# Overlapping the edges of two transformer layers: the hand-overs between tile loop, chunk loop, next layer and output

## What is computed

```
h = layernorm(x) * (1 + cb) + sb                  # x: 4 x 1024 x 256
for l in range(2):
    t = shift_token(h)                            # half of the columns come from the row before
    q, k, v = split(t @ wqkv[l])                  # 8 heads of 64, l2-normalised, scaled, rotated
    h = h + local_attention(q, k, v) @ wo[l]      # window 128: own tile of 128 rows and the one before
    t = layernorm(shift_token(h)) * lg + lb
    a, g = split(t @ w1[l] + b1[l])
    h = h + (a * gelu(g)) @ w2[l] + b2[l]
out = x + gb * h
```

## Time and profile before

| | us |
|---|---|
| median of 3 runs (2423.75 to 2428.22) | 2425.5 |
| the profiled execution: its time | 2426.99 |
| the profiled execution: its span | 2425.2 |
| TensorE busy | 2288.2 |
| VectorE busy | 1957.4 |
| ScalarE busy | 1551.4 |
| GpSimd busy | 604.0 |

### The profile page before, as it was taken

One profiled execution on the slowest core, in us unless ns is written; L12 is line 12 of the kernel. 1 busy time (PEld: TensorE's weight loads), 2 busy tenths in 40 slices (PEclk: granted clock), 3 DMA queues, 4 the chain that ended last, 5 costly groups with the idle time before them and its releaser, 6 DMA issues. The chain is left out here.

```text
span 2425.2 us, 63570 instructions
## 1 busy us (share of the span) xinstructions
PE 2288.2 (94%) x21268; PEld 1753.3 (72%) x21268; DVE 1957.4 (81%) x4606; ACT 1551.4 (64%) x3018; POOL 604.0 (25%) x692
## 2 busy tenths in 40 slices
PE   6999999999999999699999997999899999998994
PEld 4767776676777776577777776888677777776884
DVE  6999799979998998688888886666788888885666
ACT  5777577757776775377777674443677777773442
POOL 1000000000000000255555552222545454551110
PEclk9999999999999999899999998999999999998997
DMA  4000100010011001200000000001000000000004
GB/s 130 29 19 13 59 14 19 13 59 21 13 48 49 14 13 45 94 1 2 7 5 4 7 1 28 27 0 40 8 0 9 0 9 0 9 0 10 0 0 139
DMA packets 66986, 58.06 MB, mean 24 GB/s; under 512 B 3812, under 2 KB 64348, under 8 KB 66656
## 3 DMA queue, kind: packets, MB, share of 16 engines
q1 hardware_dynamic: 66912, 57.07, 7.5%
HBM read 44.47 MB, written 8.40 MB: 22 GB/s over the span
## 5 line engine op out<-in xcount | busy, mean ns | idle before, releaser
L599 ACT ACTIVATE at_p<-at_ps_s,at_shift 128x1024 f32<-128x1024 f32 (+3 forms) x384 | 335.7, 899 | 91.2 <-PE at_ps_s L800 49.9
L340 DVE TENSOR_TENSOR at_p_lo<-at_p,at_p_hi 128x1024 f16<-128x1024 f32 (+3 forms) x384 | 357.2, 951 | 5.5
L1355 ACT ACTIVATE ly_probs<-ly_masked,ly_small,ly_rq 128x256 f32<-128x256 f32 x512 | 301.4, 594 | 2.6 <-DVE ly_small L1549 1.4
L828 PE MATMUL at_ps_o<-at_v,at_p_hi 128*128 128x65 f16 x2304 | 238.1, 193 | 3.4 <-DVE at_p_lo L340 2.5
L1249 POOL TENSOR_TENSOR ly_rope_a<-ly_rope_a,ly_rope_t 128x512 f32<-128x512 f32 x132 | 168.8, 1278 | 285.5 <-DVE ly_rope_t L1517 285.5
L828 PEld LDWEIGHTS at_ps_o<-at_v,at_p_hi 128*128 128x128 f16 x2304 | 210.6, 96 | 39.7 <-issue 27.2
L829 PE MATMUL at_ps_o<-at_v,at_p_hi 128*128 128x64 f16 x2304 | 237.2, 194 | 0.0
L830 PE MATMUL at_ps_o<-at_v,at_p_lo 128*128 128x65 f16 x2304 | 236.1, 192 | 0.0
L335 DVE CAST at_p_hi<-at_p 128x1024 f16<-128x1024 f32 (+3 forms) x384 | 206.5, 556 | 25.8 <-ACT at_p L599 14.3
L1363 ACT ACTIVATE ly_operands_plain<-ly_ps 128x512 f32<-128x512 f32 x256 | 152.5, 596 | 102.5 <-PE ly_ps L1773 99.2
L830 PEld LDWEIGHTS at_ps_o<-at_v,at_p_lo 128*128 128x128 f16 x2304 | 212.4, 99 | 0.0
(11 more groups left out here) (238 smaller groups left out, 6242.2 us busy)
## 6 DMA issues: line engine op xcount, KB each, us to landing
at_w_raw<-in_Wv SPq DMA_DIRECT2D x32, 128.0 KB, 2.1
at_w_raw<-in_Wq SPq DMA_DIRECT2D x32, 128.0 KB, 2.3
at_w_raw<-in_Wk SPq DMA_DIRECT2D x32, 128.0 KB, 2.3
at_xio<-in_states SPq DMA_DIRECT2D x4, 1024.0 KB, 6.4
out_x<-x SPq DMA_DIRECT2D x4, 1024.0 KB, 9.5
out<-stream SPq DMA_DIRECT2D x4, 1024.0 KB, 7.9
ly_shifted<-stream SPq DMA_DIRECT2D x8, 508.0 KB
x<-at_xio SPq DMA_DIRECT2D x3, 1024.0 KB, 4.4
```

The lines of the kernel that those rows point to most:

```text
L340: dve.tensor_tensor(p_lo[u % P_RING][:, :, off:], probs[u % P_RING][:, :, off:], p_hi[u % P_RING][:, :, off:], ALU.subtract).then_inc(p_lo ...
L599: act.activation(probs[u % P_RING][:, :, off:], ps_s[u % 2][:, :, off:], ACT.Exp, bias=shift[:], scale=SCORE_SCALE).then_inc(exp_done, 1)
L828: pe.matmul(out, ph, ones_hi, start=(kt == 0 and t == 0), stop=False, skip_group_check=True)
L1355: step = act.activation(pr[:, j % 2, h, :], sm[:, j % 2, h, :], ACT.Exp, bias=small[:, j % 2, 1, h:h + 1], scale=rq[:, par, 2 * j + h:2 * ...
```

## The change

- The wrapped look-ahead goes: tiles 28 to 31 are written out after the loop without the work for tiles past 31 (`left` counts the tiles that follow), tiles 0 and 1 (TensorE: 0 to 3) ahead of it, the first without an output projection.
- Statistics, normalisation, transposes and the first up product of chunk 0 are put inside tiles 29 to 31; the last output projection stands inside chunk 0, between its second and third up product.
- The next layer's first transposes and projections are put inside the last chunk. Chunks 0 and 7 are written out.
- In the tile, the output projection stands ahead of the first transposes of probabilities, values 0 and 1 stand side by side, values 2 and 3 around the next tile's scores; on VectorE the reciprocals stand ahead of the keys' copy.
- A dummy exp follows the last gelu of a layer, a dummy gelu the last exp. At the start, TensorE, VectorE and ScalarE no longer wait for GpSimd's zeroing.
- `phase_output` goes. In layer 1 GpSimd gates the stream and adds the saved x per chunk, VectorE gates the down product from PSUM and adds it, and each half chunk (256 KB) is stored at once. Loads of the saved x go through a ring of three chunks. Layer 1's chunks are written out on VectorE and GpSimd.
- w1 is loaded when the last up product of the layer before is done, wo and w2 when its last down product is. Layer 1's attention weights are split in 6 pieces instead of 8.

The core of the diff (the removed `phase_output`, the indices without look-ahead, and the buffers' places are left out):

```diff
@@ TensorE, tile
-                            project(l, t + 2, par, 2)
-                            scores(l, t, 2, par)
-                            scores(l, t, 3, par)
-                            probs_T(g, 0)
-                            project_out(l, t - 1)
-                            probs_T(g, 1)
-                            project(l, t + 2, par, 1)
-                            values(g, 0, v_slots)
-                            qk_T(l, t + 1, 0)
-                            project(l, t + 2, par, 0)
-                            probs_T(g, 2)
-                            qk_T(l, t + 1, 1)
-                            stream_T(l, t + 3, 1 - par)
-                            values(g, 1, v_slots)
-                            probs_T(g, 3)
-                            scores(l, t + 1, 0, 1 - par)
-                            scores(l, t + 1, 1, 1 - par)
-                            values(g, 2, v_slots)
-                            values(g, 3, v_slots)
-                            reciprocals_T(g)
+                    if left >= 2:
+                        project(l, t + 2, par, 2)
+                    scores(l, t, 2, par)
+                    scores(l, t, 3, par)
+                    if not first:
+                        project_out(l, t - 1)
+                    probs_T(g, 0)
+                    if left >= 2:
+                        project(l, t + 2, par, 1)
+                    probs_T(g, 1)
+                    if left >= 1:
+                        after(pe, "xa_done", g)
+                        qk_T(l, t + 1, 0)
+                    if left >= 2:
+                        project(l, t + 2, par, 0)
+                    probs_T(g, 2)
+                    if left == 0:
+                        after(pe, "f_lo", nth_norm(l, 0) + 1)
+                        hidden(nth_norm(l, 0) * HT, 0, 0)
+                    values(g, 0, v_slots)
+                    values(g, 1, v_slots)
+                    if left >= 1:
+                        qk_T(l, t + 1, 1)
+                    if left >= 3:
+                        stream_T(l, t + 3, 1 - par)
+                    if left == 1:
+                        chunk_T(l, 0, bank[0:2])
+                    probs_T(g, 3)
+                    values(g, 2, v_slots)
+                    if left >= 1:
+                        after(pe, "kT_done", nth(l, t + 1) + 1)
+                        scores(l, t + 1, 0, 1 - par)
+                        scores(l, t + 1, 1, 1 - par)
+                    values(g, 3, v_slots)
+                    reciprocals_T(g)
@@ TensorE, first and last chunk
+                def first_chunk(l):
+                    n = nth_norm(l, 0) * HT
+                    hidden(n, 1, 0)
+                    project_out(l, NT - 1)
+                    hidden(n, 2, 0)
+                    after(pe, "xa_done", NT * (l + 1))
+                    hidden_out(n, 0)
+                    hidden(n, 3, 0)
+                    hidden(n, 4, 0)
+                    chunk_T(l, 1, bank[4:6])
+                    hidden_rest(n, 0)
+                    for i in range(1, HT):
+                        hidden_out(n, i)
+                def last_chunk(l):                          # ... of layer 0
+                    hidden(n, 3, par)
+                    stream_T(l + 1, 0, 0, bank[4])
+                    stream_T(l + 1, 1, 1, bank[5])
+                    hidden(n, 4, par)
+                    hidden_rest(n, par)
+                    hidden_out(n, 1)
+                    after(pe, "gl_done", n + HT - 1)
+                    project(l + 1, 0, 0, 2)
+                    hidden_out(n, 2)
+                    after(pe, "uf_done", n + HT)
+                    project(l + 1, 0, 0, 1)
+                    hidden_out(n, 3)
+                    project(l + 1, 0, 0, 0)
+                    hidden_out(n, 4)
+                    project(l + 1, 1, 1, 2)
+                    hidden_out(n, 5)
+                    after(pe, "ya_done", NCH * (l + 1))
+                    qk_T(l + 1, 0, 0)
...
@@ VectorE
+                def tile(l, t, par, w, pair, left=NT, first=False):
+                    if left >= 1:
+                        rotate_q(l, t + 1, w)
+                        normalise_keys(l, t + 1)
+                    maxima(l, t, 2, par)
+                    if not first:
+                        add_attended(l, t - 1)
+                    if left >= 1:
+                        rotate_k(l, t + 1, w)
+                    maxima(l, t, 3, par)
...
+                    if left == 0:
+                        chunk_lo(l, 0, 0)
+                    reciprocal_sums(nth(l, t), par)
+                    if left >= 1:
+                        copy_keys(l, t + 1, 1 - par)
...
+                    if left == 2:
+                        chunk_statistics(l, 0)
+                        chunk_variance(l, 0)
+                    if left == 1:
+                        chunk_shift(l, 0)
+                        chunk_normalise(l, 0)
+                    if left >= 1:
+                        maxima(l, t + 1, 0, 1 - par)
+                        maxima(l, t + 1, 1, 1 - par)
+                    normalise_out(l, t)
+                def add_hidden(l, c):                       # ... in layer 1
+                    dve.tensor_tensor(g[0], halves[0][1], gate, ALU.mult).then_inc(s["yg_done"], 1)
+                    dve.tensor_tensor(g[1], halves[1][1], gate, ALU.mult).then_inc(s["ya_done"], 1)
+                    dve.wait_ge(s["z_done"], c + 1)
+                    dve.tensor_tensor(halves[0][0], halves[0][0], g[0], ALU.add).then_inc(s["out_done"], 1)
+                    dve.tensor_tensor(halves[1][0], halves[1][0], g[1], ALU.add).then_inc(s["out_done"], 1)
@@ ScalarE, tile
+                    if left == 0:
+                        chunk_hi(l, 0, 0, bank[0:2])        # behind exps(0)
...
+                    if left == 0:                           # behind exps(3)
+                        act.activation(warm[:], expo[:, 0:1], ACT.Gelu).then_inc(s["warmed"], 1)
...
+                    if left == 1:                           # at the tile's end
+                        chunk_full(l, 0, bank[0:2])
@@ ScalarE, last chunk of layer 0, behind the last gelu
+                    act.activation(warm[:], expo[:, 0:1], ACT.Exp).then_inc(s["warmed"], 1)
@@ GpSimd, chunk, layer 1
+                    pool.tensor_tensor(rest, rest, gate, ALU.mult).then_inc(s["z_gated"], 1)
+                    pool.tensor_tensor(rest, rest, x1[:, c % X1_RING], ALU.add).then_inc(s["z_done"], 1)
@@ SyncE, behind layer 1
+                    for i in range(2):
+                        sp.wait_ge(s["out_done"], 2 * c + i + 1)
+                        sp.dma_start(rows_out(c)[:, part, :], x[:, c * CT + 2 * i:c * CT + 2 * i + 2, :]).then_inc(s["stored"], 16)
```

More of the change, by code:

```diff
@@ L1318, in _ @@
[L1318 to L1320 removed]
+                        carry_out(l, 1, 1, 1)
+                        hold(pool, s["tick"], (s["xT_mm"], at(2)))
+                        stage_tile(1, 3)
+                        add_rotated(l, 0, 1)
+                        inverse_key_norms(l, 1)
@@ new lines, in last_chunk @@
+                def last_chunk(l):
+                    n = (l * NCH + NCH - 1) * HT
+                    more = l + 1 < L
+                    for i in range(3):
+                        hidden_full(n, i)
+                        hidden_lo(n, i)
+                    hidden_full(n, 3)
+                    if more:
+                        stream_lo(l + 1, 0, 0, bank[4])
+                    hidden_lo(n, 3)
+                    if more:
+                        stream_lo(l + 1, 1, 1, bank[5])
+                    hidden_full(n, 4)
+                    hidden_full(n, 5)
+                    hidden_lo(n, 4)
+                    hidden_lo(n, 5)
+                    if not more:
+                        add_hidden(l, NCH - 1)
+                        return
+                    l = l + 1
@@ new lines, in last_chunk @@
+                    maxima(l, 0, 0, 0)
+                    maxima(l, 0, 1, 0)
+                for i in range(2):
+                    part = slice(i * A_COLS // 2, (i + 1) * A_COLS // 2)
+                    after(dve, "w_hi_done", i + 1)
+                    dve.tensor_tensor(a_lo[:, part], a_raw[:, part], f32(a_hi[:, part]), ALU.subtract).then_inc(s["w_lo_done"], 1)
+                stream_lo(0, 0, 0)
+                scale_rotations()
+                last_statistics()
+                squared_norms(0, 0, 1)
@@ new lines, in chunk @@
+                def chunk(l, c, par):
+                    ci = nth_norm(l, c)
+                    after(pe, "f_lo", ci + 1)
+                    for i in range(3):
+                        hidden(ci * HT, i, par)
+                    after(pe, "ya_done", ci)
+                    hidden_out(ci * HT, 0)
+                    hidden(ci * HT, 3, par)
+                    hidden(ci * HT, 4, par)
+                    chunk_T(l, c + 1, bank[4:6])
+                    hidden_rest(ci * HT, par)
+                    for i in range(1, HT):
```

(21 more changed lines are left out.)

832 lines of the change are left out of this document (439 added, 393 removed).

## The result

The kernel after takes 2385.4 us (median of 4 runs, 2384.2 to 2386.0), the kernel before 2424.6 in the same session: a ratio of 0.984 (95% interval 0.9825 to 0.9851), 39 us less. I had forecast 2341, with a range of 2318 to 2362. The sign is right; less than half of the gain is there, and the time lies 23 us above the range.

A forecast was written before the change was run, and what follows sets the result against it. TensorE, busy 94% of the span, was taken to bound the kernel, with idle stretches at hand-overs and the end. Terms by stretch summed to -85.2 us from 2427.0, giving 2341.8 (2340 against the median); forecast 2341, range 2318 to 2362.

The forecast's parts named there:

- start, with tile 0: Kernel start: engines no longer wait for GpSimd's zeroing, but most of the gain is lost; 1 us less, bounds 0 and 3.
- order in a tile: 58 whole tiles: eight changes of TensorE array form instead of nine, 0.16 us a tile, 9.3 us less.
- table loads: Layer 1's tile loop: ScalarE's function table load leaves the loop's body, 15 x 1.09 = 16.4 us less.
- tiles to chunks, twice: Tile 29 to chunk 0's end, each layer: 84.9 us falls by 12.5, so 25 less for two.
- layer 0 to layer 1: Start of chunk 7 to end of layer 1's tile 0: 63.9 us becomes 53.4, 10.5 less; bounds 6 and 16.
- layer 1, chunks 1 to 6: VectorE's added additions and GpSimd's passes delay the first down product: 0.35 x 7 = 2.5 us more; bounds 0 and 8.
- last chunk: Layer 1's last chunk: its look-ahead transposes go, 0.8 us less.
- end: Behind the last down product: 31.3 us becomes 6.6, 24.7 less; bounds 21 and 26.
- A: Hand-overs from tiles to chunks hide well: 24 us less a layer instead of 12.5, so 2318 us; chance 0.12.
- B: Hand-overs hide badly, or the tile order gains nothing: +7.5 us a layer and +9.3, so 2365 us; chance 0.14.
- C: The change doesn't do away with layer 1's table loads: 2341 + 16.4 = 2357 us; chance 0.05.
- D: In tiles, the ring of scores, maxima, exps, reciprocals, keys' copy becomes the bound: 15.8 us a tile, 2456 us; chance 0.03.

The follow-up runs named there:

- the loads ahead: Kernel after, with SyncE issuing the next attention weights' loads and x1's loads ahead of the last batch's copy to the shifted stream: 2348.3 us, ratio 0.969.
- the two moves here: On the loads ahead: VectorE's chunk 0 statistics behind tile 30's maxima, 2351.8 us; with GpSimd's passes early too: chunk 0's transposes at tile 30's end, 2338.8 us.

## Why the prediction was wrong

The terms of the sum against what the two traces give, from the same anchors (start of a tile's first projection, start of a chunk):

| term | forecast | measured |
|---|---|---|
| start, with tile 0 | -1.0 | 0.0 |
| order in a tile | -9.3 | -5.8 |
| table loads | -16.4 | -15.5 |
| tiles to chunks, twice | -25.0 | -21.5 |
| layer 0, chunks 1 to 6 | 0 | +15.1 |
| layer 0 to layer 1 | -10.5 | -12.3 |
| layer 1, chunks 1 to 6 | +2.5 | +25.1 |
| last chunk | -0.8 | -1.1 |
| end | -24.7 | -25.9 |
| sum | -85.2 | -41.9 |

**The step that failed** is the one on what is moved to GpSimd and SyncE. I wrote that the gates and additions "go elsewhere", to GpSimd "with 24 us of room", and counted instructions. I never asked when the operand x1 lands, nor that chunk 1 of layer 0 would come 12 us earlier than the loads that GpSimd waits for in it. Both loads stand on SyncE behind the last copy to `shifted`. The windows of the earlier trace rows don't show it, since in the kernel before TensorE did not wait; but GpSimd's timeline did, with 23.6 us of waiting for `in_qk_rows`. In the sum, layer 0's chunks 1 to 6 stand at nothing and layer 1's at +2.5. The step costs 36.2 us (17.0 and 19.2). With the loads ahead the time is 2348.3, inside the range and 7 above the forecast.

**The rest**, term by term.

- Layer 1's chunks: the place was right, and so was the rule of the Trainium skill (page "GPSIMD Engine Reference", section Specifications) that spoke against the change; the size was wrong. I took 0.35 us from one instruction stretched from 0.69 to 1.04; beside two passes back to back the stretch is 1.9 us, and the chunk 1.17 longer than layer 0's, 7 us in all. Moving the passes got it back.
- The chunks' missing 0.31 us (about 5 us) is the operands' offset, which I saw in the diff and priced at nothing.
- Order in a tile: 0.10, not 0.16. I gave every change of form the same 0.15 us. But leaving the scores costs 0.10 us ahead of the output projection (1.83 us for it, and 1.73 behind transposes) and 0.05 ahead of transposes (0.49 for 0.44): putting the projection there gives back most of the missing 0.06.
- Table loads: confirmed alone, at 16.3 us.
- End: four instructions of VectorE, and a span that ends 5.5 us behind the last product, for 6.6; 256 KB land in 2.2 us, for my 2.6.
- Hand-over to the chunks: tile 29 took 13.8 us (13.6 laid out), tile 30 21.6 and 19.8 (18.2), tile 31 17.0 and 16.8 (15.3), chunk 0 22.8 and 24.5 (23.4): the waits are where I put them, and the clock costs more than the 2 us I gave it (in tile 30 of layer 0 eight scores take 2.0 us, and 1.06 elsewhere).
- Hand-over to layer 1: 1.8 us better than laid out, a granted clock of 1.00 throughout.
- Start: TensorE was 1.6 us earlier, and tile 0 took 18.6 instead of 17.0, at a granted clock of 0.82 for 0.90. That VectorE's work for the last batch, which did not move, holds it up is likely and untested.
- The bounds: "the added bounds of the forecast alone are 2322 to 2358" does not come out of the terms. Their own bounds, added one to one, give 2303 to 2396, and the measured time lies inside; the range was narrower than the working behind it.

**Rivals.** A, B and C rested on the hand-overs and the table; none of them describes what happened. B's time is nearer, by accident. D (a ring in the tile) did not occur: the tile has no wait. But the run with the old order on TensorE alone shows how near it was: 0.3 us a tile, most likely from one late copy.

## What to carry to other kernels

When work is pulled forward, look up for each of its operands when it is issued, not only who computes it, and read the whole queue that issues it, also where its waits cost nothing now. A DMA whose issue takes 25 us is a fault even while it is free. A wait that is moved in a chain shared by three engines can come back elsewhere, and with it a lower clock: of the two moves here one cost 3.5 us, the other gained 2.9 in one layer and lost 2.5 in the other. Passes that were moved away from an instruction that TensorE waits for paid in full.

## What the runs showed of the hardware

- A copy of 127 partitions x 8 rows of 512 bytes between two SBUF tensors runs at 20 GB/s with a DMA share of 0.08, where one of 16 engines is 0.06, and the next DMA on the same queue is held for 25 us. The window of that stretch in the kernel after:

```profile
1493.00:1515.00 22.00, 22.00 (x131) 19.33 (x130) 14.46 (x36) 9.43 (x15) 0.00 (x0) 1.00 0.08 20
```

  Cut in 112 and 15 partitions it moves at 229 GB/s with a share of 0.99, and the three issues take 0.65, 1.62 and 0.77 us. The Trainium skill, page "DMA: Bandwidth & Descriptors", section Why a DMA increments its semaphore by 16 and not by 1, says that a DMA runs on the largest number of engines up to 16 that divides the slowest dimension of both its sides, and names 127 partitions as a case of one engine; the traces agree, with the shares and the rates. How long the next DMA of the queue is held is what the runs add.
- An instruction of VectorE with two inputs in SBUF took 2.61 us instead of 0.68 beside a GpSimd pass of 2.41 us, and one of four columns 1.70 instead of 0.15 beside a pass of 2.73. The Trainium skill, page "GPSIMD Engine Reference", section Specifications, names VectorE instructions with two SBUF inputs among those that contend; the trace agrees, and shows that even a small one can be held for most of a pass.
- With the buffer that is loaded as weights 64 bytes further on in each partition, a down product takes about 6 ns less (5.44 against 5.74 us for 48); with all of a chunk's operands 32 bytes further on, the 36 up products take 8.40 us instead of 8.19. The cause is open.
- The table load in the loop's body, 16.3 us over layer 1, goes away with one dummy exp ahead of the loop.
